# Attention ahead of a mixture of experts: value products in batches of three steps, with the turn of the maxima and the bank copies moved

## What is computed

```python
def reference(x, w_attn, b_attn, w_proj, b_proj, gate_w, w1, w2):   # x: 2 x 1024 x 512
    xn = layernorm(x)
    q, k, v = split(xn @ w_attn + b_attn)            # 16 heads of 32
    q, k = rope(q), rope(k)                          # rotation depends on the head
    attn = softmax(where(causal, q @ k.T, -inf)) * 512 ** -0.5
    attended = (attn @ v) @ w_proj + b_proj
    # 8 experts of 352, the best 2 per token, weights summing to one
    experts = sum_e combine[:, e] * ((silu(xn @ g_e) * (xn @ u_e)) @ w2_e)
    return x + attended + experts
```

## Time and profile before

| | us |
|---|---|
| median of 3 runs | 957.33 |
| lowest, highest | 950.41, 961.78 |
| the profiled execution | 952.79 |
| its span, first to last instruction | 950.9 |
| attention within the span | 191 to 552 |
| mean granted clock of TensorE | 0.944 |

### The profile page before, as it was taken

One profiled execution on the slowest core, in us unless ns is written; L12 is line 12 of the kernel. 1 busy time (PEld: TensorE's weight loads), 2 busy tenths in 40 slices (PEclk: granted clock), 3 DMA queues, 4 the chain that ended last, 5 costly groups with the idle time before them and its releaser, 6 DMA issues. The chain is left out here.

```text
span 950.9 us, 12387 instructions
## 1 busy us (share of the span) xinstructions
PE 853.8 (90%) x3661; PEld 527.3 (55%) x3662; DVE 365.2 (38%) x1125; ACT 289.5 (30%) x616; POOL 271.1 (29%) x352
## 2 busy tenths in 40 slices
PE   3779999389899999957999998999999999999990
PEld 3668988245555555534555443466666666666650
DVE  4972552575656666644666111111111111111110
ACT  3041131104545655534555600021222222222210
POOL 4951000305223242303323250023333333333330
PEclk9889999758979999987999999999999999999995
DMA  9286596876346676692631125826364554533326
GB/s 321 100 265 190 197 322 202 254 171 223 106 141 168 182 197 154 172 279 67 154 98 41 39 77 179 270 56 157 68 157 118 102 152 105 109 66 65 65 33 198
DMA packets 76491, 143.19 MB, mean 151 GB/s; under 512 B 12704, under 2 KB 26528, under 8 KB 76384
## 3 DMA queue, kind: packets, MB, share of 16 engines
q1 hardware_dynamic: 40272, 69.88, 23.7%
q10 hardware_dynamic: 26752, 54.09, 20.3%
q0 software_dynamic: 9424, 18.69, 10.6%
HBM read 81.21 MB, written 61.15 MB: 150 GB/s over the span
## 5 line engine op out<-in xcount | busy, mean ns | idle before, releaser
L1272 ACT ACTIVATE probs<-scores_t 128x512 f32<-128x512 f32 (+3 forms) x384 | 164.0, 492 | 163.8 <-PE scores_t L1394 149.8
L867 PE MATMUL gu<-w,rows_t 128*128 x624 | 197.4, 459 | 1.1 <-DVE o_t L833 1.1
L1414 PE MATMUL o_acc<-probs,v_ones 128*64 128x512 f32 (+3 forms) x768 | 150.2, 514 | 14.7 <-POOL probs L1217 14.7
L1371 PE MATMUL maxima<-k_stack,q_stack 96*128 96x512 f32 (+3 forms) x384 | 143.1, 393 | 15.0 <-DMA q_stack<-qk_hi 9.0
L867 PEld LDWEIGHTS gu<-w,rows_t 128*128 128x128 f32 x624 | 115.2, 190 | 69.7 <-issue 19.7
L1394 PE MATMUL scores_t<-q_stack,k_stack 98*128 98x512 f32 (+3 forms) x384 | 140.0, 390 | 4.8 <-DMA q_stack<-row_lo 2.6
L1297 DVE CUSTOM_DVE_ANT_0 masked_scores<-maxima,mask_m 128x128 f32<-128x128 f32 (+3 forms) x256 | 121.4, 485 | 25.1 <-PE maxima L1371 20.7
L1301 DVE TENSOR_REDUCE mx<-maxima 128x1 f32<-128x512 f32 x128 | 88.2, 689 | 104.4 <-PE maxima L1371 104.2
L1394 PEld LDWEIGHTS scores_t<-q_stack,k_stack 98*128 98x128 f32 x384 | 74.1, 195 | 67.7 <-issue 44.9
L885 PE MATMUL down<-w,hidden_t 128*128 (+1 forms) x234 | 107.0, 592 | 0.8 <-DVE hidden_t L841 0.8
L1371 PEld LDWEIGHTS maxima<-k_stack,q_stack 96*128 96x128 f32 x384 | 78.1, 205 | 35.9 <-DVE mx L1301 9.6
(11 more groups left out here) (148 smaller groups left out, 895.6 us busy)
## 6 DMA issues: line engine op xcount, KB each, us to landing
w<-in_w_t SPq DMA_DIRECT2D x8, 1408.0 KB, 6.5
routed<-blank_row ACTq DMA_DIRECT2D x20, 514.0 KB, 7.4
rows<-routed ACTq DMA_DIRECT2D x39, 256.0 KB
qk_hi<-st_hi SPq DMA_DIRECT2D x32, 256.0 KB, 5.1
qk_lo<-st_lo SPq DMA_DIRECT2D x32, 256.0 KB, 6.7
q_stack<-qk_hi ACTq DMA_DIRECT2D x32, 256.0 KB, 4.5
k_stack<-qk_hi ACTq DMA_DIRECT2D x26, 256.0 KB, 5.5
v_all<-o_t SPq DMA_DIRECT2D x4, 1536.0 KB, 5.7
```

The source lines that it names most:

```text
L867: last = nc.tensor.matmul(gu[r][j][:, 0:I], rows_t[r][:, k * P:(k + 1) * P], w1[:, bass.ds(e, 1), k, j * I:(j + 1) * I].rearrange("p o n - ...
L1272: nc.scalar.activation(probs[:, k % PR, h, 0:w], scores_t[e % RING][:, 0:w], ACT.Exp).then_inc(exp_done, 1)
L1371: nc.tensor.matmul(mb[at % RING][:, 0:w], q_st[i][0:3 * HD, h, t * P:(t + 1) * P], k_st[i][0:3 * HD, h, c * CH:c * CH + w], start=True, st ...
L1414: last = nc.tensor.matmul(o_acc[c][2 * HD * h:2 * HD * (h + 1), CH - w:CH], v_st[i][:, j, h:h + 2, :].rearrange("p o d -> p (o d)"), probs ...
```

## The change

`BATCH` goes from 2 to 3. With it, and without a line of their own in the diff, `NB` goes from 6 to 4 blocks a round, `PER` from 4 to 6 pairs a block, `PR` from 4 to 6 steps of probabilities. `LEAD` 39 and `TURN_LAG` 2 put the turn at slot 11, the last pair of the second block (scores 6 to 8), ahead of that pair's unit; the round's last unit is at slot 8 of the same block. `LOW_LAG` 0 puts `row_low` on VectorE behind that same slot's unit. The copy of half 1 of the round before stands behind exponential 5 (was 3), the copy of half 0 of this round behind exponential 11 (was 7). In the new order the blocks of a round hold scores 3 to 5, 6 to 8, 9 to 11, and 0 to 2 of the next round, and behind them the value steps 0 to 2, 3 to 5, 6 to 8, 9 to 11. SyncE's, GpSimd's and the loads' order are as before.

```diff
-    LEAD = 36
+    LEAD = 39
     TURN_LAG = 2
-    LOW_LAG = 1
+    LOW_LAG = 0
...
-    BATCH = 2
+    BATCH = 3
     NB = NS // BATCH
     PER = NU // NB
...
                     if k == 2 * BATCH - 1 and n:
                         stage_bank(n - 1, NC - 1)
-                    if k == TPC + 2 * BATCH - 1:
+                    if k == 4 * BATCH - 1:
                         stage_bank(n, 0)
```

## The result

| | before | after |
|---|---|---|
| median, us | 956.5 (4 runs) | 1004.2 (4 runs) |
| lowest, highest | 950.4, 961.8 | 1000.4, 1006.5 |
| span of the profiled execution | 950.9 | 1004.7 |
| first unit to last value product | 191.7 to 551.4 (360 us) | 193.3 to 603.8 (410 us) |
| mean granted clock | 0.944 | 0.928 |

The ratio is 1.050, with a 95% interval of 1.042 to 1.057. The time lies in the range, but not at the forecast of 1050: it lies where I had put the rival "the clock holds" (1004), and not for that rival's reason.

What follows compares the result with a forecast made beforehand. PE, busy 90% of the span, was taken to bound the kernel. From 952.8 us: + 5 blocks + 60.2 stops - 2.6 old row waits + 45.5 clock - 3.6 residual - 7.4 VectorE wait = 1050 us; range 995 to 1095.

Steps and rivals of the forecast that it cites:

- the clock holds: Rival, chance 0.22: PE's stops in attention come as forecast but cost no clock; 1004 us, within 990 to 1020.
- What bounds: PE, busy 90% of the span; the change touches attention alone, where a steady round has almost no wait.
- Part 1: Attention rounds of four blocks instead of six save two turns between kinds of product, 0.92 us a round.
- end just in time: In six-pair blocks, ScalarE's exponentials (0.48 us each at 512 columns) would free the scores' three banks in time.
- my three pieces of it: Turn cost in a block: about 0.13 us at the first S, 0.15 before the first V, 0.16 in V.
- Part 2: Six-pair blocks wait for VectorE to empty three banks: +0.33 us a round, 5 us in fifteen.
- Part 3: SyncE's row DMAs stand behind the late bank copy; PE stops 4.3 us ahead of score 0, 14 times, 60.2 us.
- the bound of 3.9 us: Lower bound of PE's stop ahead of score 0, with a row landing of 4.2 us.
- Part 4: Behind nearly every stop in attention the granted clock falls to 0.50: 13 times 3.5 us, 45.5 us.
- Part 5: Other attention waits: residual -3.6 us, VectorE's at 260 us with its half clock -7.4, LEAD 39 and LOW_LAG 0 about 0.
- The residual's wait: PE's 14.7 us wait for mask 8 of round 9, behind the residual load, claimed to shrink by 3.6 us.
- The slack of the scaling: GpSimd's scale step before mask 8: slack of 2 us and more, so 0; 2 us in seven rounds if gone.

Runs made afterwards that it cites:

- experiments 6 and 7: VectorE reducing only every fourth column: on the kernel before, 943.4 us (0.992); on the changed kernel with rows(n + 1) ahead of sort_out(n, 0), 953.0 us (1.000).
- experiments 1 and 2: Changed kernel with rows(n + 1) ahead of sort_out(n, 0): 960.0 us; kernel before with only the copy of half 0 moved behind exponential 11: 1028.3 us.
- experiment 5: Changed kernel with four more 64 KB DMAs on SyncE between sort_out(n, 0) and rows(n + 1): 1042.6 us, 1.094.
- experiment 9: Changed kernel with rows ahead of sort_out and GpSimd's scaling of a finished span behind mask 11 instead of at step 5: 951.7 us, 0.999.
- experiment 4: Changed kernel with the last query and key piece (256 KB each) issued behind the bank copy at exponential 11, right ahead of the rows: 1020.0 us, 1.071.
- experiment 2: Kernel before, blocks of two steps, with only the copy of half 0 moved from behind exponential 7 to behind exponential 11: 1028.3 us, 1.081.
- experiment 8: Changed kernel with rows ahead of sort_out, and HIGH_STEP 9, LEAD 36 and LOW_LAG 1 as before: 966.0 us, 1.013.

## Why the prediction came out as it did

**What bounds, and where it goes.** Right. The loss is in attention (50 of the 54 us of span), in PE's waits.

**Part 1, fewer turns, 0.92 us a round.** The step that was wrong as a gain. V gave its 0.3 us; the rest never came, even with VectorE out of the way (experiments 6 and 7). There the scores' three banks hold the six-pair blocks in its place; that they account for all of the missing 0.6 us is argued from the starts, not shown. I had written that the exponentials "end just in time"; they are some tenths late. The 0.46 us of a turn was not firm either: my three pieces of it add up to 0.44, and the block of the earlier trace rows leaves 0.53.

**Part 2, six pairs in a block.** Right in mechanism and nearly in size: S and U stretches of 2.79, 3.33, 2.74 and 2.92 us in place of 2.74, 3.20, 2.67 and 2.89. With V a round is 20.19 us: 22.27 from score 0 to score 0, less the stop of 2.08. The sum had 19.82, and the kernel before 19.49. That is ten us in all instead of five.

**Part 3, the late copy.** Right in the place, the cause and the count of the stops, which experiments 1 and 2 show from both sides. The term of the sum that was mis-sized is the last link: rows to score 4.5 us by the prediction, 2.5 us measured in eleven of fourteen rounds, so stops of 2.1 us, not 4.3, and 30.3 us in all, not 60.2. The earlier trace rows gave a price under load, and I carried it to a place where the load was nearly over (the value piece landed at most 1.5 us after the issue of the rows that took 2.5 us); the bound of 3.9 us was made from the same place. The loads' places (the last key piece behind exponential 9, right ahead of the rows before and 4.2 us ahead of them after) were there to be read.

**Part 4, the clock.** What I took from the earlier trace rows holds for the stop I forecast: in experiment 5, with stops of mostly 4 us, the clock fell 14 times of 14. With the real ones it fell six times of fourteen, and twice of eight at 2.1 us. Against undisturbed rounds, with the waits taken off, the six spells and the one at the residual's wait cost 20 us, and the two of before 8: 12 us net, instead of 45.5 - 6. The price of a spell was 2.8 us (2.3 to 2.5 for those of 6.8 us), not 3.5. The idle stretch of 2.6 us that left the clock at 1.00 in the kernel before (579.4) is a thin support for a rival too: in the changed kernel the clock fell behind the same wait, now at 634 us. That the rival "the clock holds" has the measured number is chance: it had stops of 4.3 us at no clock cost, and what took place is half the stop and a third of the clock. The Trainium skill, "TensorE: Matmul & The Clock Gate", section on oscillation in real kernels, tells of a kernel in which each group behind a DMA wait starts at the low clock, and lays it to the length of that wait, a condition that I had left out. Experiment 5's stops of 4 us agree with it, and six of eight stops of 2.1 us, which kept the clock, show that the condition is needed.

**Part 5.** The residual's wait shrank by 2.1 us (14.7 to 12.6) instead of 3.6. The wait at 260 us went below my 1 us, to 0.3. The slack of the scaling, which I had put at 2 us and more, was used up: four waits of 0.7 to 1.6 us, 4.3 in all; in the changed kernel they cost little, because the stop behind three of them shrinks from 2.1 to 0.9 us, and they came to light at full price once the rows were first (6.2 us in that trace, and gone in experiment 9). LEAD 39 put the first score 1 us later behind the first unit (20.4 against 19.4 us), and the last rounds did not give it back in full.

Put together, with what the trace of after has in place of each term: 952.8 + 10 (blocks) + 27.7 (stops, 30.3 - 2.6) + 2.2 (masks, with the residual) - 2.3 (VectorE) + 12 (clock) + 1 (ahead of the first score) = 1003.4. The profiled execution of after took 1006.5; the other 3 us lie outside attention, where nothing was changed.

**The experiment that settles it.** With the rows no longer late, the masks no longer behind the scaling, and nothing else changed back (experiment 9), the kernel is level with before. So nearly all of the 48 us was waiting that the moved copies made, with its clock. Level does not mean that blocks of three are free: their rounds are 0.6 us longer there too, 8 to 9 us in all, and shorter waits pay for it (the residual's 10.1 us instead of 14.7, the one for VectorE at 260 us 1.1 instead of 2.4, with 3.4 us of low clock behind it instead of 13.7).

## What to carry to other kernels

A copy that is moved also moves the DMAs behind it on another engine's queue, and everything that stands behind those: write the queue down and ask what the next wait in it holds back. The time from a DMA's issue to its use is a price of its place; before it is carried to another, look at which transfers were in flight where it was read. And before a block is made longer, compare its length with the depth of every ring that feeds or drains it: here three banks for six products ate more than the 0.92 us of saved turns, 1.0 us a round on VectorE (1.5 against 0.5) and up to 0.6 on ScalarE. Whether deeper rings would give it back was not tried.

## What the runs showed of the hardware

Two 8 KB DMAs issued back to back were usable 2.5 us after the first issue when no larger transfer was in flight, or one that landed within 1.5 us. They took 3.3 to 4.1 us when a 256 KB piece had been issued on another queue some 2.1 us before (experiment 4). In the kernel before, with such a piece 1.2 us ahead and one of 384 KB 1.6 us behind, it was 4.7 to 4.8 us in three of the four rounds in which PE waited, and 5.7 in the other.

The granted clock fell behind all eleven stops of 3.8 to 5.7 us in experiment 5, behind nine of ten of 3.0 us in experiment 2, and behind two of eight of 2.1 us in the changed kernel. It also fell behind two short waits close together (1.55 and 0.90 us with 1.1 us of work between), and in experiment 8 behind two of its fourteen single waits of 0.9 us in attention. The spells at 0.50 lasted 3.4 to 13.7 us, though PE had work all the time once the stop was over. One of 6.8 us cost the changed kernel 2.3 to 2.5 us, less than half of its length.
